# Output projection and last stage of an attention-plus-FFN kernel: Wout loaded by SyncE in f32 and cast on ScalarE, last stage's loads issued two tiles ahead

## The reference

```
x = L0_attn_x                                   # [4, 2048, 2048]
xn = _layernorm(x, axis=-1)
s = _L0_attn_ref(xn, g_norm, Wq, Wkv, Wout, g_out)
g = _silu(_L0_ffn_ref(xn, w_gate, w_up, w_down))
x = x + s * g
...
# _L0_attn_ref, its end
out = jnp.einsum('bhij,bjd->bhid', attn, v)
out = out.transpose(0, 2, 1, 3).reshape(B, N, HEADS * DIM_HEAD)
out = out @ Wout
return _layernorm(out, g_out)
```

## Time and profile before

| | us |
|---|---|
| time, median of 2 runs | 6424.02 |
| lowest, highest | 6392.01, 6456.03 |
| profiled execution, device time | 6472.99 |
| its span on the slowest core (core 3), on the fastest | 6471.2, 6357.3 |
| PE, DVE, ACT, POOL busy | 2873.7, 2934.0, 1841.6, 177.3 |
| stretch from the first `ao_scr` store to the last (core 3) | 6033.4 to about 6303.5 |
| last stage (core 3) | 6304 to 6471 |

### The profile page before, as it was taken

One profiled execution on the slowest core, in us unless ns is written; L12 is line 12 of the kernel. 1 busy time (PEld: TensorE's weight loads), 2 busy tenths in 40 slices (PEclk: granted clock), 3 DMA queues, 4 the chain that ended last, 5 costly groups with the idle time before them and its releaser, 6 DMA issues.

```text
span 6471.2 us, 47104 instructions; the slowest of 8 cores (6357.3 to 6471.2 us)
## 1 busy us (share of the span) xinstructions
PE 2873.7 (44%) x14544; PEld 1369.2 (21%) x14544; DVE 2934.0 (45%) x2997; ACT 1841.6 (28%) x1849; POOL 177.3 (3%) x165
## 2 busy tenths in 40 slices
PE   2222212215777777777700000006666656664660
PEld 1210000002333333333300000003222222332220
DVE  5652322365666565566586656754233320001105
ACT  0004444523333333333201211133233222653010
POOL 0000000000000000000001111120000000000000
PEclk6555555557887787778755555556787878997665
DMA  3127777722222222222111121125566643000335
GB/s 105 59 49 229 220 246 246 259 96 100 98 98 98 98 98 98 98 98 98 72 55 39 42 62 52 39 65 177 184 218 207 202 168 106 1 1 7 48 61 203
DMA packets 350714, 727.78 MB, mean 112 GB/s; under 512 B 151426, under 2 KB 251906, under 8 KB 292868
## 3 DMA queue, kind: packets, MB, share of 16 engines
q1 hardware_dynamic: 282356, 706.96, 31.6%
q0 software_dynamic: 68112, 17.83, 3.0%
HBM read 658.64 MB, written 83.89 MB: 115 GB/s over the span
## 4 chain that ended last, share of the span: by engine, by line
PE 31%; DVE 27%; DMA 23%; issue 11%; ACT 6%; DVEq 1%; SPq 0%; ACTq 0%; POOL 0%; POOLq 0%
PE psA L729 9%; PE psB L729 7%; DMA AB<-y_scr 6%; DVE AF L806 3%; DVE AF L804 3%; DMA g_scr<-AF 3%; ACT AB L1043 3%; DVE AB L350 3%; DMA AF<-y_scr 3%; DMA ao_scr<-AF 3%; PE psA L993 2%; PE psU L347 2%; PE psB L993 2%; DMA AF<-Wg 2%; DMA AF<-Wu 2%
## 5 line engine op out<-in xcount | busy, mean ns | idle before, releaser
L374 ACT ACTIVATE AF<-AF,negh,rmB 128x2048 f32<-128x2048 f32 x192 | 401.1, 2089 | 759.8 <-DVE AB L382 389.6
L380 DVE TENSOR_TENSOR AF<-AF 128x2048 f32<-128x2048 f32 x192 | 438.7, 2285 | 342.9 <-ACT AF L377 342.9
L729 PE MATMUL psA<-AB 128*128 128x512 bf16 x2048 | 584.8, 456 | 0.0
L729 PE MATMUL psB<-AB 128*128 128x512 bf16 x2048 | 491.6, 402 | 0.0
L534 ACT ACTIVATE AF<-AF 128x2048 f32<-128x2048 f32 x192 | 366.5, 1909 | 348.8 <-DVE wsum L537 220.2
L838 PE MATMUL psA<-sid,zs_tm 128*1 128x128 f32 x8 | 3.0, 371 | 925.2 <-DVE zs_tm L835 925.2
L993 PE MATMUL psA<-AB 128*128 128x512 bf16 x1024 | 345.5, 423 | 148.3 <-DMA AB<-y_scr 147.5
L347 PE MATMUL psT<-sid,AB 128*128 128x128 bf16 x1664 | 166.1, 260 | 532.9 <-DVE AB L350 395.3
L377 ACT ACTIVATE AF<-AF,posh,rmB 128x2048 f32<-128x2048 f32 x192 | 399.2, 2079 | 0.0
L347 PE MATMUL psU<-sid,AB 128*128 128x128 bf16 x1792 | 210.9, 290 | 379.7 <-DVE AB L441 267.7
L993 PE MATMUL psB<-AB 128*128 128x512 bf16 x1024 | 340.4, 417 | 0.0
(11 more groups left out here) (172 smaller groups left out, 4436.0 us busy)
## 6 DMA issues: line engine op xcount, KB each, us to landing
AF<-Wg SPq DMA_DIRECT2D x128, 1024.0 KB, 6.3
AF<-Wu SPq DMA_DIRECT2D x128, 1024.0 KB, 8.2
AF<-Wd SPq DMA_DIRECT2D x128, 1024.0 KB, 8.4
AB<-y_scr SPq DMA_DIRECT2D x256, 512.0 KB, 4.5
y_scr<-AF SPq DMA_DIRECT2D x64, 512.0 KB, 3.0
AF<-y_scr SPq DMA_DIRECT2D x32, 1024.0 KB, 5.7
AF<-x_own SPq DMA_DIRECT2D x16, 1024.0 KB, 8.9
y_scr<-AB SPq DMA_DIRECT2D x32, 512.0 KB, 3.8
```

The costliest lines, as they stand in the source:

```text
L374: E(S, lambda s: s.activation(g1[:, 0:Wn], src_ap, AF.Sign, bias=negh[:, 0:1], scale=rmB[:, mcol:mcol + 1]), reads=[src_key, "negh", "rmB" ...
L380: E(V, lambda v: v.tensor_add(g1[:, 0:Wn], g1[:, 0:Wn], g2[:, 0:Wn]), reads=[g1k, g2k], writes=[g1k], tag=f"tadd{tag}")
L729: E(T, lambda t, c=c, ns=ns, buf=buf, mi=mi, pdst=pdst: t.matmul(pdst[:, ns * ST:(ns + 1) * ST], wtT[:, buf, mi, c, :], iaT[:, c, ns * ST: ...
```

## The change

There are two edits and a larger buffer. In the first, `ldwo` no longer uses GpSimd's queue. The block is loaded by SP, in f32, into a new double buffer `wq_stg`, and ScalarE casts it into `wq_slab2` (tag `cwo`). The calls of `ldwo` stay where they were. In the second, the last stage is cut into `p3_front` (three loads and the statistics) and `p3_tail` (the passes and the store). The fronts of tiles 0 and 1 are written first, and then tail of tile tt, front of tile tt + 2, and so on. `stile` becomes double, for which the f32 arena grows from 21760 to 22528 elements per partition.

```diff
+        wq_stg = AFa.alloc(2 * DC * 128, (2, DC, 128))
+
         def ldwo(oc):
-            DMA("gpsimd", 2 + oc % 2, wq_slab2[:, oc % 2, :, :],
+            DMA("sync", 12 + oc % 2, wq_stg[:, oc % 2, :, :],
                 Wout[:, oc * 128:(oc + 1) * 128].rearrange("(c p) m -> p c m", p=128),
-                writes=[("wq", oc % 2)], tag=f"ldwo{oc}")
+                writes=[("wqs", oc % 2)], tag=f"ldwo{oc}")
+            E(S, lambda s, oc=oc: s.copy(wq_slab2[:, oc % 2, :, :], wq_stg[:, oc % 2, :, :]),
+              reads=[("wqs", oc % 2)], writes=[("wq", oc % 2)], tag=f"cwo{oc}")
...
-        stile = AFa.alloc(D)
+        stileD = AFa.alloc(2 * D, (2, D))
...
-        for tt in range(TT):
+
+        def p3_front(tt):
...
             ln_stats(("aot", tt % 2), aot[:, tt % 2, :], f"l3_{tt}", tt % 2)
...
+        def p3_tail(tt):
+            stile = stileD[:, tt % 2, :]
+            sk = ("stile", tt % 2)
...
+        p3_front(0)
+        if TT > 1:
+            p3_front(1)
+        for tt in range(TT):
+            p3_tail(tt)
+            if tt + 2 < TT:
+                p3_front(tt + 2)
```

More of the change, by code:

```diff
@@ L287, in build_program @@
             I + I + 3 * S_own + 256 + 2 * S_own,
-            10 * D,
+            11 * D,
             4 * S_own + 2 * ST + 2 * S_own)
@@ L1139, in build_program @@
             ln_stats(("aot", tt % 2), aot[:, tt % 2, :], f"l3_{tt}", tt % 2)
[L1140 to L1145, removed]
+        def p3_tail(tt):
+            stile = stileD[:, tt % 2, :]
+            sk = ("stile", tt % 2)
+            E(V, lambda v, tt=tt, stile=stile: v.tensor_scalar(stile, aot[:, tt % 2, :],
+                                                               rstd[:, tt % 2:tt % 2 + 1],
+                                                               mbv[:, tt % 2:tt % 2 + 1],
+                                                               ALU.mult, ALU.add),
+              reads=[("aot", tt % 2), ("rstd", tt % 2), ("mbv", tt % 2)], writes=[sk], tag="ln3ap")
+            E(V, lambda v, stile=stile: v.tensor_mul(stile, stile, goB),
+              reads=[sk, "goB"], writes=[sk])
+            E(V, lambda v, tt=tt, stile=stile: v.tensor_mul(outt[:, tt % 2, :], stile, grb[:, tt % 2, :]),
+              reads=[sk, ("grb", tt % 2)], writes=[("outt", tt % 2)], tag="sg")
             E(V, lambda v, tt=tt: v.tensor_add(outt[:, tt % 2, :], outt[:, tt % 2, :], xrb[:, tt % 2, :]),
```

## The result

The changed kernel takes 6513.28 us (median of 11 runs, 6456.93 to 6577.22) where the kernel before takes 6445.54 (10 runs, 6376.73 to 6560.35). The ratio is 1.013, with a 95% interval of 1.008 to 1.018: longer by 83 us (51 to 117), which is clear of the noise but under 2%. The ratio is taken over the executions without a lowered clock on one die (6505.73 is the median of nine such here), while the two medians above are of all executions and lie 68 us apart. I had forecast +37 us, 6461, with a range up to 6512.

What follows compares the result with a forecast made beforehand. The prediction took the projection loop to be bound by SP's chain of 128 stores, with PE's round almost level. +41 us there and -4 in the last stage gave +37 on 6424, hence 6461 us, range 6402 to 6512.

Steps and rivals of the forecast that it cites:

- The bound of the loop: Projection loop before: a chain of 128 stores, 270.1 us, with PE's round of 17.2 us per group almost level.
- The stop: Projection loop, eighth store to next group's first: issue, landing, cast, copy in a row, 9.1 us where 1.65 was, thirteen times.
- The landing: Projection loop: a 1 MB f32 load of Wout lands in 6.0 us, bounds 5.5 and 7.5, upward 10.4.
- the term of the seven stores: Projection loop: the other seven stores of a group take 7 x 1.65 us, giving 20.6 us per block with the 9.1.
- slowed stores: Projection loop before: 59 us of the store chain were stores slowed by a load or waiting a little for data.
- The last stage: Last stage: tails stay 20.1 us apart, only the ends differ (+7.5 and -11.4); together -4 us, bounds -6 and -1.
- The sizing of tail 0: Last stage: the first tail waits for tile 1's statistics and begins 20 us after the start, not 12.4.
- The sum: Whole kernel: +41 us in the projection loop and -4 in the last stage give +37 us.
- A: Projection loop: load and cast hide under the matmuls, PE's round carries the loop; -3 us, 6417 in all; chance 0.12.
- B: Projection loop: low clock stretches PE's round to 22.2 us and makes it the bound; +67 us, 6487 in all; chance 0.18.
- C: Last stage: loads run ahead of statistics, tiles about 13 us apart; -42 us, 6419 in all; chance 0.06.
- D: Projection loop: Wout landings of 13.0 us or more make the kernel slower by over 2%; 6565 at 14 us; chance 0.04.

Runs made afterwards that it cites:

- the half load: Changed kernel loading only the first 8 of 16 chunks of each Wout block from block 2 on; store stretch 291.6 us against 322.3.
- The probe: Changed kernel without Wout loads after the first two, half the matmuls, transposes and copies in fours, statistics at the tail's head; store stretch 220.0 us.
- the repeated run: Changed kernel unaltered, run again beside the kernel before in a later session; 6493.85 us against 6446.56, ratio 1.007.
- the last version: Kernel before with stores unchained, statistics at the tail's head, transposes grouped with one copy per group, Wout on GpSimd's queue; 6195.19 us against 6466.06, ratio 0.956.

## Why the prediction was wrong, point by point

*The bound of the loop* was read rightly for seven of the eight cores: a chain of 128 stores on SP. On core 3 itself the chain ran over PE's round until 6134.94, and that round of 17.2 us belongs to a core whose matmuls were the slowest of the eight (medians 10.2 us for 32 there, 8.8 to 10.0 on the others); it was not the round of the kernel in general. The experiment with the load one block earlier, where the chain of core 7 is nothing but stores, shows the chain of stores again.

*The stop* was forecast at 9.1 us. Over twelve groups of the changed kernel's core 0 it is 8.8 to 9.7, with a mean of 9.0. The landing, taken as 6.0 from a load of equal pieces, has a median of 6.3; the cast, 1.9 from a pass of the same width, took 1.90. No stop is hidden, and that the landing counts thirteen times is shown by the half load (31 us for 2.1 us less).

*What failed is the term of the seven stores*: 7 x 1.65 = 11.6 us, "the sum already has all stores at 1.65". On core 0 the group is 21.58 us in the mean of twelve (from 5975.32 to 6234.26), so the seven stores take 12.6, 1.80 each. 1.65 was the spacing of core 3's ordinary stores (median 1.66 in its chain) and not a mean over all. On core 0 the ordinary spacing is 1.70, and single stores of 1.8 to 2.9 us, at any place of a group, add 0.7 us per group. The probe, with 1.73 in the mean, says that 0.6 of the 1.0 us is there without any load of Wout; what makes the rest is not shown. Over thirteen groups this is 13 us, and in the last sixteen stores 3 more (29.7 us in place of 26.4), on the core whose stretch is the longest; in the mean of the cores the stretch is 3 us shorter. If a store cost 1.73 in the kernel before too, only 48 of its 270 us were slowed stores, not 59; less could be gained back by keeping load and stores apart than I reckoned. The sum was +41; the store stretch grew by 55.1.

*The last stage* was forecast at -4, with -6 to -1. It is -6.9 in the profiled pair and -7 in the repeated run. Part of this is scatter of the old stage: the run with the first edit alone, whose last stage is the old one, has 168.5 and not 170.0, and the other runs with the new stage have 164.0 to 166.9, which would make it -2 to -5, within the bounds. The sizing of tail 0 was right in kind (18.6 us after the start where I took 20), and the tails are 20.0 apart as forecast. That the statistics block a ready tail is shown by the experiment that moves them.

*The sum*: +37 was forecast; the two stages changed by +48, and the repeated comparison gave +45. The first comparison gave +83 by its ratio and +68 between its medians, and its 6513.28 lies 1.3 us outside the range; the repeated one, 6493.85, lies inside, so on which side of the bound the time fell was also a matter of scatter. The seven stores account for 14 us of the miss and the last stage for 3 the other way. Another 21 us are the base: I added to 6424, and the kernel before came to 6445 to 6474 when it was run more often. The range took the spread of two runs as that of the base. With the 20 us of the first comparison's medians that are in neither stage, and stay open, these make up the 52 us between 6461 and 6513.

*The rivals.* A (the load hides, as the Trainium skill's page "DMA: Bandwidth & Descriptors", section "Issuing engines are not separate DMA queues", would have it) did not happen, but its price was right: with the cast on GpSimd or the load one block earlier the loop is at 269 and 265. These two runs agree with the rule, since the load stays on SP in both. The cost came from what waits behind the load on an in-order engine, of which that section says nothing. B (PE's round as the bound) did not happen: the first copy follows the cast at once, and the 32 matmuls took 8.7 to 9.9 us on core 0 and not 13.7. C (an overlapping last stage) needed one more edit, and is worth 49 us with it. D did not happen; the pieces of Wout, 8 KB apart, land in 6.3 us.

## What to carry to other kernels

Moving a load to another queue cost nothing here as long as nothing ready stood behind it (264.7 and 269.4 us against 268.3), and its whole latency thirteen times where something did: ask what stands in front of its issue, and what stands behind the instruction that waits for it. An operation that waits for a fresh load (a cast, statistics) belongs behind all work that is already ready on its engine; both edits broke this, one for +55 us and one for 49 us not gained. Where one name stands for a whole DRAM tensor or a whole PSUM tile, its stores and transposes form a chain of latencies. For the stores a name for each part was worth more here than the better place of the load: it took 80 us from the store stretch of the changed kernel, the place 58. For the transposes, own names and fewer copies were only tried together.

## What the runs showed of the hardware that I had not expected

A store of 64 KB in 512-byte pieces takes 1.58 to 1.62 us as a rule, and in the mean 1.73 with its hand-over, even when no load of Wout is about. A cast of 128x2048 from f32 to bf16 took 1.89 us on GpSimd and 1.90 on ScalarE; I had taken it at twice that on GpSimd. The same 32 matmuls took very different times. On core 3 before they took 10.2 us in the median, behind eight transposes with pauses of mostly 0.61 us. In the changed kernel they stand behind the same pauses, and on core 0 they took 8.7 to 9.9:

```profile
6076.70 8.84 PE L1110 MATMUL psA<-AB 128*128 128x512 bf16 x32
```

In the last version, without pauses, they took 8.56 on core 0 and 7.07 on core 2, at mean granted clocks of 0.83 and 0.99 over their store stretches. So the pauses alone do not set the time of the matmuls, and what does is not shown. I had expected 13 to 14.5 us for a group of the last version, and it took 10.1 on core 0.
